# Layer 2's opening makes the keys and values of batches 1 to 3 beside batch 0's gathers; two more gather turns in the expert stage

## The chip, the cores and the metric

One core of a Trainium2 chip runs the whole program. The metric is the device time of one execution in microseconds. Engines: TensorE (PE) multiplies and transposes, VectorE (DVE) and ScalarE (ACT) do elementwise work and reductions, GpSimd (POOL) issues the indexed DMAs and small arithmetic, SyncE (SP) issues plain DMAs. Each engine works through its own queue in program order and waits on semaphores.

## The reference, cut to what matters

Two layers over x of shape (8, 256, 512), with a context of the same shape:

```python
x = x + tanh(g_xattn[0]) * causal_attention(layernorm(x), ctx, ctx)
x = x + tanh(g_ffn[0])   * mixture_of_32_experts_top8(layernorm(x))
# layer 2
q = rms_norm(layernorm(x) @ w_q.T + b_q, g_q)       # needs layer 1's x
k = rms_norm(ctx @ w_k_img.T + b_k_img, g_k_img)    # needs only ctx
v = ctx @ w_v_img.T + b_v_img                       # needs only ctx
x = x + tanh(g_xattn[1]) * (softmax(q k / sqrt(32)) v @ w_o.T + b_o)
x = x + tanh(g_ffn[1])   * (layernorm(x) @ ternary(w).T + bias)
```

In layer 2 only the 257 image tokens of the context count, so all 256 are keys and the text branch has none. There are 16 heads of 32. The point that matters here: keys and values of layer 2 depend on the context alone, queries depend on the rows that the experts produce.

## The kernel before, in words

The program has three stages, each a block; all engines meet at the end of a block (L1114, the exit of the expert stage's block).

1. Layer 1's attention and gating, batch by batch, up to about 341 us.
2. The expert stage (`experts`), up to 962.3 us: 160 tiles of 128 rows, each loaded from `x_slots`, multiplied by its expert's weights and stored to `y_tiles` in DRAM. At its end POOL starts to collect batch 0's expert rows (`add_first`): for each of a token's 8 experts one indexed DMA per 128 tokens (t = 0, 1), which adds the rows to `xs` (even turns) or to a second buffer `odd` (odd turns). A turn waits for the tile stores that it may read. Turns 0 to 3 are in the expert stage's block, turns 4 to 7 (`LAST_ADDS = 4`) open layer 2's block.
3. Layer 2 (`layer1` in the code), batch by batch, with attention written as 16 steps (two heads of one query tile in each). Work of other batches is hung beside the steps by tables that name, for each engine, which piece comes after which step: `PREP1` for the preparation of the next batch, `POST1` for the end of the batch before. Batch 0's own preparation has no attention to hide beside; its order on each engine is `BEGIN1`. I call the time from the block's start to the first attention step the opening, and the 16 steps of batch n body n.

The pieces of a preparation: `sc` splits the context into two fp16 halves, `T0 T1` transpose them on PE (16 fp16 transposes for two, L1548), `P...` are products of 12 matmuls of 128x512 (L1542) into one bank, read by DVE (L1659): keys, values, queries, for two row tiles each. `xc` is the mean and variance of the batch's rows on DVE (L1636 to L1642) and the inverse root on POOL (L1615); `xn` normalises on DVE (L1646); `sx T2 T3` split and transpose the result. `P` on ACT squares keys or queries for their RMS norm and on POOL makes the factor (L1622 to L1626), `r` scales queries (L1666), `k0..k3` split into head parts, `S0..S7` transpose them to the attention's layout (L372, copied L379). `v` is a wait only.

POOL's queue in layer 2 is in program order too: `BEGIN1["pool"]` with some of batch 1's gathers between, then in body n one gather of batch n+2 after each step (`add_rows`), and the small pieces at their steps. A gather of one t waits for the landing of the gather before it of the same t, since both add to the same rows; each t has eight in a batch. `xc` of batch n+1 stands at step 4 of body n on DVE and 5 on POOL, and waits for all gathers of batch n+1.

```python
            before = {"P1": 4, "xc": 0, "P3": 4}
            for piece in BEGIN1["pool"]:
                add_next(before[piece])
                pool_prep(pool, b0, piece)
            add_next(2 * ROWS - added[0])
```

## Time and profile before

| | |
|---|---|
| device time, median of 3 runs | 1558.1 us (1552.81 to 1558.12) |
| span of the profiled execution | 1525.3 us; its own device time is not in the records, the median lies 32.8 us above the span |
| PE, DVE, ACT, POOL busy | 86%, 64%, 60%, 34% of the span |
| mean granted TensorE clock | 0.939 |
| expert stage ends | 962.3 us |
| opening of layer 2 | 962.4 to 1022.0 us |
| body 0, 1, 2, 3 | 57.5, 62.3, 62.6, 62.4 us |

A share of busy time is a mean over stages with different limits; the opening and the bodies have to be read by themselves. The granted clock says at which of its two levels TensorE ran (1.00 is 2.4 GHz, 0.50 is 1.2 GHz).

### The profile page before, as it was taken

To read this page: it belongs to the slowest core of one execution; us is meant where nothing else is said; L and a number is where in the kernel's file an instruction comes from. 1 tells how busy PE (TensorE), PEld (TensorE's weight loads), DVE (VectorE), ACT (ScalarE), POOL (GpSimd) and SP (SyncE) were. 2 spreads that over 40 slices of the span, in tenths; PEclk is the share of its full clock that TensorE was granted. 3 is DMA by queue.
4 is the path that set the end of the run, shared out by engine and by line. 5 is a ranking of instruction groups with operands and counts; after the bars stand their busy time and mean duration, and the time that the engine had idled before them with its cause. 6 is when DMAs were issued, how large, how long until landed. Compare 5 with 4: busy or idle time off the path is not lost.

```text
span 1525.3 us, 37150 instructions
## 1 busy us (share of the span) xinstructions
PE 1309.4 (86%) x10733; PEld 834.6 (55%) x10734; DVE 972.8 (64%) x2387; ACT 920.1 (60%) x2261; POOL 520.1 (34%) x531
## 2 busy tenths in 40 slices
PE   5888888837999999999999999477989889898984
PEld 3656655524556666665666666144556555555552
DVE  5888888755456665655655633255787777776853
ACT  4777777724556666666666666244766667667661
POOL 1044444455333433332000001665554444541000
PEclk9988888968999999999999999688999999999997
DMA  2044344458888767767676545775654555642000
GB/s 72 29 173 180 146 146 151 156 213 304 269 285 282 256 219 261 238 217 244 218 242 222 181 149 154 126 111 83 98 99 65 104 82 84 100 65 52 15 1 28
DMA packets 96131, 233.39 MB, mean 153 GB/s; under 512 B 11808, under 2 KB 11808, under 8 KB 91424
## 3 DMA queue, kind: packets, MB, share of 16 engines
q0 software_dynamic: 33712, 113.79, 29.8%
q1 hardware_dynamic: 62320, 118.34, 23.3%
q8 instruction: 55, 0.90, 0.3%
q14 instruction: 44, 0.36, 0.1%
HBM read 140.84 MB, written 91.24 MB: 152 GB/s over the span
## 4 chain that ended last, share of the span: by engine, by line
PE 45%; DMA 9%; DVE 9%; issue 8%; ACT 3%; POOL 3%; SPq 1%; DVEq 0%; ACTq 0%; POOLq 0%
PE bank L1305 18%; PE bank L1329 10%; PE bank L1542 6%; DMA xs<-y_tiles,slot_ix 5%; PE bank L1293 4%; PE bank L258 2%; PE bank L1316 1%; PE bank L278 1%; DMA xg<-x_slots 1%; DVE l_nmax L325 1%; PE bank L1548 1%; POOL xs L430 1%; DMA x_slots<-blank 1%; DVE l_stack L379 1%; PE bank L240 1%
## 5 line engine op out<-in xcount | busy, mean ns | idle before, releaser
L1305 PE MATMUL bank<-wh,xT 128*128 x1280 | 343.3, 330 | 4.7 <-DVE hp L1420 4.4
L430 POOL DMA_INDIRECT xs<-y_tiles,slot_ix x120 | 194.6, 1622 | 234.2 <-DMA y_tiles<-ysb 99.1
L293 ACT ACTIVATE l_probs<-bank,l_bias 128x256 f32<-128x256 f32 (+1 forms) x512 | 224.4, 449 | 64.4 <-DVE l_bias L327 64.0
L1305 PE MATMUL bank<-wl,xT 128*128 x640 | 211.4, 330 | 0.0
L325 DVE TENSOR_REDUCE l_nmax<-bank 128x2 f32<-128x512 f32 (+1 forms) x256 | 158.1, 617 | 70.8 <-PE bank L240 41.3
L1410 DVE SCALAR_TENSOR_TENSOR hv<-bank,sg 128x192 f32<-128x192 f32 x160 | 56.9, 356 | 227.5 <-ACT sg L1364 203.5
L1379 ACT ACTIVATE ysb<-bank,xg 128x512 f32<-128x512 f32 x160 | 109.9, 687 | 119.1 <-PE bank L1329 119.1
L305 ACT ACTIVATE l_probsT<-bank 128x512 f32<-128x512 f32 (+1 forms) x256 | 140.0, 547 | 65.6 <-PE bank L278 65.2
L1358 ACT ACTIVATE xT<-bank 128x1024 f16<-128x1024 f16 x160 | 162.5, 1016 | 15.0 <-PE bank L1293 14.8
L1305 PEld LDWEIGHTS bank<-wh,xT 128*128 128x128 f16 x1280 | 126.5, 99 | 81.3 <-issue 11.1
L1329 PE MATMUL bank<-wh,hT 128*128 x480 | 156.1, 380 | 0.9 <-issue 0.9
L240 PE MATMUL bank<-l_stack 128*128 128x256 f16 (+1 forms) x512 | 105.7, 275 | 59.1 <-ACT l_probs L293 49.3
L278 PE MATMUL bank<-id,l_probs 128*128 128x128 f32 x896 | 149.7, 286 | 2.1 <-ACT l_probsT L305 0.5
L699 POOL DMA_INDIRECT x_slots<-room,slot_ix x112 | 113.4, 1013 | 108.3 <-issue 47.0
L1542 PE MATMUL bank<-w_hi,halfT 128*128 128x512 f16 x384 | 125.9, 390 | 18.9 <-DVE accb L1659 17.1
L1200 POOL DMA_DIRECT2D raw<-in_experts_dram x30 | 16.8, 560 | 334.1 <-DVE wl L1436 333.8
L1364 ACT ACTIVATE sg<-bank 128x192 f32<-128x192 f32 x160 | 52.8, 330 | 113.8 <-PE bank L1305 113.8
L1329 PE MATMUL bank<-wl,hT 128*128 x320 | 121.4, 379 | 0.0
L1293 PEld LDWEIGHTS bank<-id,xg 128*128 128x128 f16 x1280 | 84.9, 99 | 58.7 <-DMA xg<-x_slots 22.6
L1293 PE MATMUL bank<-id,xg 128*128 128x128 f16 x1280 | 98.9, 221 | 19.1 <-DMA xg<-x_slots 18.9
L278 PEld LDWEIGHTS bank<-id,l_probs 128*128 128x128 f32 x896 | 102.6, 147 | 11.7 <-ACT l_probsT L305 7.4
L1436 DVE SCALAR_TENSOR_TENSOR wl<-raw,wh x64 | 95.4, 1491 | 20.0 <-issue 15.9
(246 smaller groups left out, 2538.1 us busy)
## 6 DMA issues: line engine op xcount, KB each, us to landing
xg<-x_slots SPq DMA_DIRECT2D x160, 272.0 KB, 2.8
y_tiles<-ysb SPq DMA_DIRECT2D x160, 256.0 KB, 2.5
raw<-in_experts_dram POOLq DMA_DIRECT2D x30, 1280.0 KB, 7.1
x_slots<-blank SPq DMA_DIRECT2D x33, 272.0 KB, 3.6
xs<-in_x_dram SPq DMA_DIRECT2D x8, 512.0 KB, 4.4
cbuf<-in_ctx_dram SPq DMA_DIRECT2D x8, 512.0 KB, 5.8
stage<-in_mats_dram POOLq DMA_DIRECT2D x4, 1024.0 KB, 7.8
room<-in_ctx_dram SPq DMA_DIRECT2D x8, 512.0 KB, 4.6
```

Of the source, the lines that this page charges most:

```text
L240: last = self.nc.tensor.matmul(o, self.stack[:, b.par, 0, h, qt * P : (qt + 1) * P], self.stack[:, b.par, 1, h, 0:nk], start=True, stop=no ...
L278: last = self.nc.tensor.transpose(self.pT[s % len(self.pT)][:, (2 * kt + u) * P : (2 * kt + u + 1) * P], self.probs[:, s % 2, u, kt * P : ...
L293: last = self.nc.scalar.activation(self.probs[:, s % 2, u, 0:nk], self.pS[s % 2][:, u * S : u * S + nk], ACT.Exp, bias=self.bias[:, s % 4, ...
L305: self.nc.scalar.activation(self.probsT[:, s % 2, 0:w], self.pT[s % len(self.pT)][:, 0:w], ACT.Copy).then_inc(self.probsT_made, 1)
L325: self.nc.vector.tensor_reduce(self.nmax[:, s % 4, :], v, AX, ALU.max).then_inc(self.max_made, 1)
L430: return nc.gpsimd.indirect_dma_start(to, None, self.y_tiles[0 : (MT + 1 - k) * P, :], ix, compute_op=ALU.add)
L699: nc.gpsimd.indirect_dma_start(shared.x_slots, bass.IndirectOffsetOnAxis(ap=slot_ix[:, QT * b.n + t, k % TOPK : k % TOPK + 1], axis=0), xe ...
L1293: last = nc.tensor.transpose(o[:, c * P : (c + 1) * P], rows[:, c * P : (c + 1) * P], id16[:])
L1305: last = nc.tensor.matmul(bGU[t.place % 2][:, 0:GU], xT[:, t.place % 2, xo + c * P : xo + (c + 1) * P], wp[:, bass.ds(w, 1), c * GU : (c + ...
L1329: last = nc.tensor.matmul(bY[t.place % 2][:, :], h, wp[:, bass.ds(w, 1), at : at + H].rearrange("p a w -> p (a w)"), start=k == 0, stop=k ...
L1358: nc.scalar.activation(xT[:, t.place % 2, :], bX[t.place % 2][:, :].bitcast(F16), ACT.Copy).then_inc(x_ready, 1)
L1542: last = nc.tensor.matmul(o, xT[:, xo + c * P : xo + (c + 1) * P], w[:, c * H : (c + 1) * H], start=n == 0, stop=n == len(todo) - 1)
```

## The change

Layer 2's opening gets six row tiles of batches 1 to 3 (`EARLY = 3`): SP loads their context, ACT and DVE split it (`c0..c5`), PE transposes it (`t0..t5`) and makes the key product (`x0..x5`) and the value product (`v0..v5`) of each in banks of their own, DVE adds the bias, SP stores both to a DRAM tensor `kv`. In the preparation of batches 1 to 3 (`PREP1_EARLY`) the pieces `sc T0 T1` and four of six products go; SP loads the raw keys into `cbuf` and the values into `vbuf`, ACT squares the keys from there (`s0 s1`). Batch 0's order (`BEGIN1`) is rewritten, `xc` moves on DVE behind `v2`, and on POOL behind `P1`. `LAST_ADDS` goes from 4 to 2: turns 4 and 5 of batch 0's gathers stand in the expert stage's block. Three reads of table values in the expert stage get bounds.

```diff
-LAST_ADDS = 4
+LAST_ADDS = 2
+EARLY = 3
 BEGIN1 = dict(
-    pe=["T0", "T1", "P0", "P1", "T2", "T3", "P2", "P3", "S0", "S1", "S2", "S3", "S4", "S5", "P4", "S6", "S7", "P5", "v"],
-    act=["sc", "T0", "T1", "sx", "P0", "P1", "T2", "T3", "k0", "k1", "P2", "P3", "k2", "k3"],
-    pool=["xc", "P1", "P3"],
-    dve=["sc", "xc", "xn", "P0", "sx", "P1", "P2", "k0", "k1", "P3", "S0", "S1", "S2", "S3", "r", "k2", "k3", "S4", "S5", "P4", "S6", "S7", "P5"])
+    pe=["T0", "T1", "P0", "P1", "t0", "P2", "P3", "t1", "x0", "v0", "t2", "S0", "S1", "S2", "S3", "x1", "v1", "t3", "x2", "v2",
+        "T2", "T3", "x3", "P4", "P5", "v3", "t4", "x4", "v4", "t5", "S4", "S5", "x5", "S6", "S7", "v5", "v"],
+    act=["sc", "T0", "T1", "c0", "c1", "P0", "P1", "t0", "t1", "c2", "k0", "k1", "t2", "c3", "t3", "sx", "T2", "T3", "c4", "c5",
+         "P4", "P5", "t4", "k2", "k3", "t5"],
+    pool=["P1", "xc", "P5"],
+    dve=["sc", "c0", "c1", "P0", "P1", "P2", "P3", "k0", "k1", "c2", "x0", "v0", "S0", "S1", "S2", "S3", "x1", "c3", "v1", "x2", "v2",
+         "xc", "xn", "sx", "x3", "c4", "P4", "P5", "v3", "c5", "r", "k2", "k3", "x4", "v4", "S4", "S5", "x5", "S6", "S7", "v5"])
+PREP1_EARLY = dict(
+    pe={6: ["T2"], 7: ["T3", "P0"], 8: ["<S0", "<S1"], 9: ["<P1", "<S2"], 10: ["S3"], 12: ["S4", "S5"], 13: ["S6", "S7"], 15: ["v"]},
+    act={1: ["s0"], 2: ["s1"], 4: ["sx"], 6: ["T2"], 7: ["k0", "T3"], 8: ["k1", "P0"], 9: ["P1"], 10: ["k2"], 11: ["k3"]},
+    pool={5: ["xc"], 6: ["s1"], 11: ["P1"]},
+    dve={4: ["xc", "xn"], 6: ["sx"], 7: ["k0", "P0"], 8: ["k1", "S0", "S1"], 9: ["P1", "S2"], 10: ["S3", "r", "k2"],
+         12: ["k3", "S4", "S5"], 13: ["S6", "S7"]})
...
-                code = pe.value_load(t_pe[0:1, t.column()])
+                code = pe.value_load(t_pe[0:1, t.column()], min_val=0, max_val=E * E)
...
+            if piece[0] == "t":
+                pe.wait_ge(early_half, u + 1)
+                if u > 0:
+                    pe.wait_ge(early_copied, u)
+                turn16(bEarlyT, early16[:, u % 2, :, :]).then_inc(early_ps, 1)
+            else:
+                m = "xv".index(piece[0])
+                pe.wait_ge(early_copied, u + 1)
+                if u > 0:
+                    pe.wait_ge(kv_made, 2 * u + m - 1)
+                products(bEarly[m][:, :], earlyT[:, u % 2, :], 2 * m).then_inc(kv_ps, 1)
...
+            if piece[0] == "c":
+                dve.wait_ge(early_hi, u + 1)
+                v.scalar_tensor_tensor(early16[:, u % 2, 1, :], early_x[:, u % QT, :], SC_C, early16[:, u % 2, 0, :],
+                                       ALU.mult, ALU.subtract).then_inc(early_half, 1)
+            else:
+                m = "xv".index(piece[0])
+                dve.wait_ge(kv_ps, 2 * u + m + 1)
+                if u > 0:
+                    dve.wait_ge(kv_out[m], 16 * u)
+                v.scalar_tensor_tensor(early_out[:, m, :], bEarly[m][:, :], 1.0 / (SC_C * SC_W), vec[:, 2 * m, :],
+                                       ALU.mult, ALU.add).then_inc(kv_made, 1)
...
+            def load(n):
+                sp.wait_ge(at.parts_ready, 4 * n)
+                if early(n):
+                    for m in range(2):
+                        sp.wait_ge(kv_out[m], 16 * QT * n)
+                    sp.dma_start(cbuf[:, :, :], kv[n - 1, 0]).then_inc(ctx_in, 16)
+                    if n >= 2:
+                        sp.wait_ge(at.out_made, 2 * (n - 1))
+                    sp.dma_start(vbuf[:, n % 2, :, :], kv[n - 1, 1]).then_inc(v_in, 16)
+                else:
+                    sp.dma_start(cbuf[:, :, :], cv[n]).then_inc(ctx_in, 16)
...
-            before = {"P1": 4, "xc": 0, "P3": 4}
+            before = {"P1": 0, "xc": 0, "P5": 4}
...
+            pe.wait_ge(early_copied, EARLY_TILES)
+            pe.wait_ge(kv_made, 2 * EARLY_TILES)
```

The last two waits stand between the opening and the first attention step. SP issues all twelve stores and waits for them before its loads of the bodies.

## Rows read from the trace of the kernel before

**Rows 1.** The page: span and busy time of PE.
```profile
span 1525.3 us, 37150 instructions
PE 1309.4 (86%) x10733; PEld 834.6 (55%) x10734; DVE 972.8 (64%) x2387; ACT 920.1 (60%) x2261; POOL 520.1 (34%) x531
```
**Rows 2.** Windows: stretch, length, busy PE PEld DVE ACT POOL, clock, DMA share, GB/s.
```profile
962.36:1022.20 59.84, 30.23 (x175) 15.72 (x176) 23.86 (x42) 14.65 (x29) 37.01 (x30) 0.71 0.70 112
1022.20:1079.70 57.50, 47.14 (x405) 30.05 (x404) 34.96 (x72) 35.14 (x103) 33.31 (x26) 0.91 0.63 96
1079.70:1142.00 62.30, 55.99 (x478) 34.52 (x476) 46.51 (x92) 41.16 (x111) 33.78 (x27) 1.00 0.56 87
1142.00:1204.60 62.60, 56.36 (x472) 35.10 (x473) 46.25 (x93) 40.81 (x111) 29.27 (x25) 0.97 0.53 85
```
**Rows 3.** POOL's gathers in time order: start, length, [idle before <- releaser].
```profile
959.80 1.53 POOL L430 DMA_INDIRECT room<-y_tiles,slot_ix  x1 [0.30 <-issue]
976.50 1.53 POOL L430 DMA_INDIRECT room<-y_tiles,slot_ix  x1 [0.30 <-issue]
986.62 1.58 POOL L430 DMA_INDIRECT xs<-y_tiles,slot_ix  x1 [0.18 <-issue]
1024.66 2.03 POOL L430 DMA_INDIRECT xs<-y_tiles,slot_ix  x1 [0.52 <-DMA xs<-y_tiles,slot_ix]
1030.82 1.55 POOL L430 DMA_INDIRECT xs<-y_tiles,slot_ix  x1 [1.78 <-ACT l_probs L293]
1042.22 1.55 POOL L430 DMA_INDIRECT xs<-y_tiles,slot_ix  x1 [1.74 <-DMA xs<-y_tiles,slot_ix]
1081.17 1.85 POOL L430 DMA_INDIRECT xs<-y_tiles,slot_ix  x1 [1.11 <-ACT l_probs L293]
```
**Rows 4.** The exit of the expert stage's block: instructions, first and last start.
```profile
L1114 PEldq EVENT_SEMAPHORE  x2: 51/51/51, 960.4 to 962.3; - x2
L1114 POOLq EVENT_SEMAPHORE  x2: 17/17/17, 962.2 to 962.2; - x2
```
**Rows 5.** PE in time order, opening and body 0.
```profile
965.06 1.89 PE L1548 MATMUL bank<-id,l_parts 128*128 128x128 f16 x16 [4.82 <-DVE l_parts L1653]
992.68 1.06 PE L1548 MATMUL bank<-id,l_parts 128*128 128x128 f16 x16
995.29 0.39 PE L1542 MATMUL bank<-w_hi,halfT 128*128 128x512 f16 x1 [1.55 <-ACT halfT L1593]
997.68 0.38 PE L1542 MATMUL bank<-w_hi,halfT 128*128 128x512 f16 x1
998.93 0.38 PE L1542 MATMUL bank<-w_hi,halfT 128*128 128x512 f16 x1 [0.87 <-DVE accb L1659]
1047.76 0.60 PE L240 MATMUL bank<-l_stack 128*128 128x256 f16 x2 [8.31 <-ACT l_probs L293]
```
**Rows 6.** DVE in time order: normalisation, first reciprocal of a body's end.
```profile
982.29 0.69 DVE L1862 TENSOR_TENSOR xs<-xs,room 128x512 f32<-128x512 f32 x1 [1.28 <-DMA room<-y_tiles,slot_ix]
986.48 1.06 DVE L1646 TENSOR_SCALAR accb<-xs,mv,rstd 128x512 f32<-128x512 f32 x2 [0.85 <-POOL rstd L1615]
1044.57 1.05 DVE L1646 TENSOR_SCALAR accb<-xs,mv,rstd 128x512 f32<-128x512 f32 x2 [8.31 <-POOL rstd L1615]
1094.95 1.00 DVE L1646 TENSOR_SCALAR accb<-xs,mv,rstd 128x512 f32<-128x512 f32 x2 [1.87 <-POOL rstd L1615]
1155.32 1.06 DVE L1646 TENSOR_SCALAR accb<-xs,mv,rstd 128x512 f32<-128x512 f32 x2
```
**Rows 7.** DMA issues from 940 us on: KB each, median us to landing.
```profile
out_dram<-outb SPq DMA_DIRECT2D x8, 512.0 KB, 2.8
room<-in_ctx_dram SPq DMA_DIRECT2D x7, 512.0 KB, 4.3
```
**Rows 8.** The bounded read of a table value on SP; PE's tile products.
```profile
L1157 SPq FUSED_REGOPS  x280: 46/152/162, 342.1 to 939.2; - x140
...
L1305 PE MATMUL bank<-wh,xT 128*128 x1280 | 343.3, 330 | 4.7 <-DVE hp L1420 4.4
```

More of the change, by code:

```diff
@@ L1633, in dve_prep_ @@
             if piece == "xc":
+                if early(b.n):
+                    chain.batch(b.n)
                 for t in range(QT):
@@ L1774, in load_next @@
-            def load_next(b):
-                sp.wait_ge(at.parts_ready, 4 * b.n + 4)
-                load(b.next())
-            sp.sem_inc(out_free, 1)
-            load_next(Batch(0, 0, 0))
-            load_next(Batch(1, 1, 0))
-            with sp.Fori(0, (B - 3) // 2) as i:
-                for k in range(2):
-                    load_next(Batch(2 * i + 2 + k, k, i + 1))
-                    store(Batch(2 * i + k, k, i))
-            for n in range((B - 3) // 2 * 2, B):
+            kv = shared.kv.rearrange("e m (t p) h -> e m p t h", p=P)
@@ new lines, in load_early, with store_early, store @@
+            def load_early(i):
+                if i > 0:
+                    sp.wait_ge(early_half, QT * i)
+                sp.dma_start(early_x[:, :, :], cv[i + 1]).then_inc(early_in, 16)
+            def store_early(u):
+                for m in range(2):
+                    sp.wait_ge(kv_made, 2 * u + m + 1)
+                    sp.dma_start(kv[u // QT, m][:, u % QT, :], early_out[:, m, :]).then_inc(kv_out[m], 16)
+            def store(n):
+                sp.wait_ge(out_ready, 2 * n + 2)
+                sp.dma_start(ov[n], outb[:, :, :]).then_inc(out_stored, 16)
+                sp.wait_ge(out_stored, 16 * n + 16)
+                sp.sem_inc(out_free, 2)
@@ L1788, in _ @@
+            load_early(0)
+            for i in range(EARLY):
+                if i + 1 < EARLY:
+                    load_early(i + 1)
+                for u in range(QT * i, QT * i + QT):
+                    store_early(u)
+            for m in range(2):
+                sp.wait_ge(kv_out[m], 16 * EARLY_TILES)
+            sp.sem_inc(out_free, 1)
+            load(1)
+            load(2)
+            for n in range(B):
                 if n + 3 < B:
-                    load_next(Batch(n + 2, n % 2, n // 2 + 1))
@@ L1790, in _ @@
-                store(Batch(n, n % 2, n // 2))
+                    load(n + 3)
+                store(n)
         @block.gpsimd
@@ L1817, in body @@
                         pool_post(pool, b.prev(), piece)
-                    for piece in pieces(PREP["pool"], s) if prep else []:
+                    for piece in pieces(prep_of(b.next())["pool"], s) if prep else []:
                         pool_prep(pool, b.next(), piece)
@@ L1840, in body @@
                         act_post(act, b.prev(), piece)
-                    for piece in pieces(PREP["act"], s) if prep else []:
+                    for piece in pieces(prep_of(b.next())["act"], s) if prep else []:
                         act_prep(act, b.next(), piece)
@@ L1878, in body @@
                         dve_post_(dve, b.prev(), piece, post)
-                    for piece in pieces(PREP["dve"], s) if do_prep else []:
+                    for piece in pieces(prep_of(b.next())["dve"], s) if do_prep else []:
                         dve_prep_(dve, b.next(), piece, prep)
```

162 lines of the change are left out of this document (106 added, 56 removed).

## The prediction

> **What bounds the kernel now.** I read the page, then windows of the third stage, then POOL, PE and DVE there in order of time. Over the span PE is busy 86% [rows 1], but not evenly. In bodies 1 and 2 it is busy 56 of 62.5 us at full clock [rows 2]: they are bound by PE's work. In the opening it is busy 30.2 of 59.8 us, part of that at the lower clock [rows 2], and body 0 has a hole: PE waits 8.3 us until 1047.8 [rows 5]. The hole comes from POOL. DVE has waited 8.3 us for `rstd` when it normalises batch 1 at 1044.57 [rows 6], and POOL stood in its queue behind gathers. So there are two resources: PE's work, and POOL's chain of gathers. That chain has its own pace. Batch 1's first gather goes at 986.62, the first of its last pair at 1024.66, seven pairs later [rows 3]: 5.43 us a pair, whatever PE does, since a gather waits for the landing of the one before it on the same rows.
>
> The change takes work from the first resource where it binds. I ask what it does to the second.
>
> **Unit prices.** A warm product of 12 matmuls runs from 995.29 to 997.68 for 11 starts, so 2.4 + 0.2 = 2.6 us; the next starts at 998.93, 0.9 us after the bank is read by DVE [rows 5]. Two turns take 1.06 us warm and 1.89 us at the lower clock [rows 5]; I take 0.53 each. Early work per batch: 2 turns and 4 products, 1.1 + 10.4 = 11.5 us; for three batches 34.4 us. It is taken from bodies 0, 1, 2 and put into the opening.
>
> **Start of the block.** Turns 4 and 5 are four more gathers on POOL at 1.53 + 0.30 us [rows 3]; they follow the one that ends at 961.3, so POOL is through at 968.7. Now all engines meet at the block's exit: PE comes at 960.4 and leaves at 962.3 with POOL [rows 4]. After the change they all wait for POOL. Its sequencer may reach the exit before its last gather is through, so the price lies between 0 and 7; I take 6: the block starts at 968.4. Batch 0's rows are not sooner complete for it, as POOL issues the same eight gathers back to back until 978.0 either way [rows 3].
>
> **To the normalisation of batch 0.** PE began 2.7 us after the block's start (965.06 [rows 5]), so 971.1. DVE's order puts `xc` behind `v2`, and PE must first do 6 turns (3.2), 10 products (26.0) and S0 to S3 (2.1): 31.3 us. To it come the lower clock after the pause (the pair of turns at 965.06 cost 1.89 for 1.06 and the first product went at that clock too: 3 us) and 3 us of gaps at single banks, three of the 0.9 kind. `v2` ends at 1008.4. DVE reads it (0.7) and needs 0.7 + 4.2 us for `xc` (982.29 to 986.48 [rows 6], and the first of the two additions): `xn` begins at 1014.1 instead of 986.5. Batch 1's first gather stands behind that on POOL: +27.7 us.
>
> **To the first attention step.** T2 can begin 2.4 us after `xn`, at 1016.5. PE has idled 8 us, so I charge 2.5 us of lower clock again. Then 4 turns (2.1), 8 products x3, P4, P5, v3, x4, v4, x5, v5 (20.8), S4 to S7 (2.1), the first scores (0.9), and gaps 3.0: 31.4 us. Attention starts at 1047.9 for 1022.0: +26. So 34.4 us of work went into an opening with some 30 us of idle PE, and most of it shows, because the order has new waits and the block starts later.
>
> **Batch 1's gathers and body 0.** On POOL four gathers follow `xc`, then comes `P5`, which waits for the squares of batch 0's queries. Those need T2, T3, x3, P4, P5 on PE, from 1016.5 about 12.3 us, and 1.5 us on DVE and ACT: POOL is past it at 1031.7, and the gather chain has stood still some 5 us. Twelve gathers remain, six pairs: the last pair begins at 1031.7 + 5 x 5.43 = 1058.9. Before, the first gather of body 0 came 6.2 us after the last pair's first (1024.66, 1030.82), step 4's at 1042.22, 11.4 us later, and `xn` 2.35 us after that [rows 3, 6]. The same steps now give 1065.1, 1076.5 and 1078.8. `xn` of batch 1 is 34.3 us later. After it the body took 1079.7 - 1044.6 = 35.1 us, and of its work only one product goes (the others stood before the hole): end at 1111.3, **+31.6 us**. The late start of the bodies costs nothing more, this wait is longer.
>
> **Bodies 1 and 2.** Eleven us each go from PE. But POOL is level with PE at the start of body 1 (1081.17 against 1079.7), and `xn` came at +15.25 in that body, pinned by the gathers (DVE waited for `rstd` [rows 3, 6]). Five gathers and `rstd` need the same 15 us again, a little later for the shorter body 0 (+0.7). Only work behind `xn` gives time back: two products and small things, 5.7 us. Body 1: -4.9. In body 2 POOL had got ahead; `xn` came at +13.3 [rows 6]. It gets less ahead when body 1 is shorter; I take +11.2, so 2.1 before and 5.7 behind `xn`: -7.8. Body 3 onward is as before.
>
> **The rest.** SP's 12 stores: a store lands in 2.8 us [rows 7], and the two products of a tile lie 5.2 us apart, so the next write of the buffer doesn't wait. The last store and the load of batch 1's keys (2.8 + 4.3 us [rows 7]) end about 6 us after attention starts; ACT, whose `s0` stands at step 1, waits for them with its exponentials queued behind. This hides under the wait for `xn`; without that cover it would cost 5 us. Later loads are issued half a body ahead. The final store of batch 0 waits behind a load that waits for body 1's end: 3 us late, with most of a body until its buffer is wanted. Bounds on the table reads: on SP such a read has a register operation of 152 ns [rows 8]; PE waited only 4.7 us before 1280 tile products, so its sequencer runs ahead. I take 0; the bound is 160 x 0.15 = 24 us, and below zero nothing is removed.
>
> **Sum.** 31.6 - 4.9 - 7.8 = +18.9 us. On the span 1525.3 that is 1544.2; what lies around the span (32.8 us against the median) stays, so **1577 us** against a median of 1558.1. Own range: the block's start -6 to +1, the clock and gaps of the opening -4 to +4, the pairs' pace 5.0 to 5.9 us over six pairs -3 to +3, what bodies 1 and 2 give -8 to +5: about 1563 to 1589.
>
> **Rivals.**
> Gathers keep up, PE binds alone (faster). If POOL's chain has reserve, body 0's hole closes (8.3 us) and all 34.4 us leave the bodies, while the opening, PE-bound from 965 with 22 + 34.4 us of work and 9 us of clock and gaps, ends at 1030.5, +8.5. That is -34, 1524 us. It decides at `xn` of batch 1: it must come within 10 us of the first attention step. For it: PE idles half of the opening. Against it: the pair's pace and the waits for `rstd` [rows 3, 6]. The Trainium skill's Perfetto Trace Analysis (Identifying Performance Opportunities, Optimization Strategy) says that where the most contended engine changes over time, interleaving those regimes may help; this change does just that, and by that rule this rival is the one to bet on. The trace agrees that there are two regimes, but shows the gathers still running under the bodies. Chance 0.07.
>
> Late start, all given back (no change). The opening goes as I say, pairs run at 5.0 us (-5), and bodies 1 and 2 give the full 11.4 us each: 31.6 - 5 - 22.8 = +4, 1562 us. For it: POOL was ahead of PE by body 2. Against: body 1 began level. Chance 0.10.
>
> The sequencers are late in the expert stage. If half of the 24 us for bounds shows in the 160 tiles, 1589 us; all of it 1601. For it: PE and DVE read a value in every tile. Against: no PE gaps there [rows 8]. Chance 0.08.
>
> The forecast keeps 0.75. A measurement of this kernel tells about 0.5% (8 us) from no change. Faster is the first rival, 0.07; within 0.5% the second, 0.10; slower 0.83. For 8 in 10 the range starts at the second rival, 1562, and ends a little past the third's half price, 1590.
>
> **What would show it.** The trace after should have: PE, ACT and DVE leaving the block's exit near 968 with POOL; `xn` of batch 0 near 1014; the first attention step near 1048; a PE hole of some 20 us in body 0 ended by `rstd`, with `xn` of batch 1 near 1079; body 0 ending near 1111; bodies 1 and 2 of 57 and 55 us; bodies from 3 on at 62 us; an expert stage of unchanged pace. If `xc` of batch 0 is ready well before 1008, or body 0 has no hole, or bodies 1 and 2 fall to 51 us, the forecast is wrong in that step. If the exit waits for nothing on POOL, everything is about 6 us earlier.

## The result: 44 us slower, 2.8%

| | before | after |
|---|---|---|
| median of the runs | 1558.0 us (1552.8 to 1558.1, 4 runs) | 1602.2 us (1592.8 to 1608.1, 4 runs) |
| ratio after to before | | 1.0285, 95% interval 1.0252 to 1.0317 |
| profiled execution: span | 1525.3 us | 1601.3 us (its own time 1603.1) |

The direction was forecast, the size was not: 1577 us, with a range up to 1590. To read the spans: layer 1's stage took 341 us in the profiled execution of before and 374 us in that of after, with the same code. Of the kernels below, the four of group 2, all on one chip, show about 340 us and all others 370 to 377. In after the device time lies 1.8 us above its span, so before's span of 1525.3 belongs to a time near 1527, and not, as the prediction took it, to 1558 with 32.8 us around it. The slip cancels, since the forecast is a difference. By stages, each from its own trace (a body ends at DVE's reciprocal):

| stage, us | before | after | difference | forecast |
|---|---|---|---|---|
| layer 1 (same code) | 341.3 | 374.4 | +33.1 | 0 |
| expert stage with its exit | 621.1 | 631.0 | +9.9 | +6.0 |
| layer 2's start to the end of body 0 | 117.3 | 146.4 | +29.1 | +25.6 |
| body 1 | 62.3 | 63.4 | +1.1 | -4.9 |
| body 2 | 62.3 | 58.1 | -4.2 | -7.8 |
| bodies 3 to 6 | 242.7 | 249.4 | +6.7 | 0 |
| body 7 and tail | 78.2 | 78.5 | +0.3 | 0 |

Without layer 1 the differences make +42.9 us; the medians differ by 44.2.

The page of after, to be held against [rows 1]:

```profile
span 1601.3 us, 37800 instructions
...
PE 1329.1 (83%) x10733; PEld 844.4 (53%) x10734; DVE 975.4 (61%) x2387; ACT 924.0 (58%) x2261; POOL 518.0 (32%) x531
```

Windows of after (columns as in [rows 2]): the opening up to batch 0's normalisation and from there to the first attention step, body 0, body 1 in three parts (up to its normalisation, the 15 us behind it, the rest), body 2, body 3.

```profile
1005.40:1050.80 45.40, 34.24 (x200) 17.14 (x200) 18.99 (x33) 13.21 (x19) 9.79 (x11) 0.88 0.43 109
1050.80:1085.00 34.20, 27.96 (x166) 14.58 (x167) 16.54 (x28) 10.82 (x22) 17.53 (x14) 0.89 0.60 110
1085.00:1151.80 66.80, 39.31 (x341) 26.34 (x340) 31.07 (x66) 32.45 (x100) 36.71 (x29) 0.77 0.68 113
1151.80:1168.10 16.30, 8.08 (x82) 5.33 (x80) 7.28 (x19) 8.51 (x25) 9.12 (x7) 0.88 0.64 115
1168.10:1183.00 14.90, 12.34 (x95) 8.05 (x96) 9.45 (x19) 10.63 (x27) 8.97 (x8) 0.79 0.64 89
1183.00:1215.20 32.20, 27.72 (x241) 17.74 (x238) 25.97 (x50) 18.42 (x53) 13.92 (x13) 0.95 0.53 84
1215.20:1273.30 58.10, 47.46 (x408) 30.86 (x408) 42.63 (x86) 38.66 (x108) 30.14 (x25) 0.94 0.60 102
1273.30:1334.20 60.90, 54.90 (x472) 34.33 (x472) 46.02 (x92) 40.70 (x110) 29.28 (x25) 1.00 0.53 87
```

And two windows of before, body 1 ahead of its normalisation and behind it:

```profile
1079.70:1095.00 15.30, 14.47 (x127) 9.19 (x126) 9.70 (x23) 10.29 (x26) 9.17 (x7) 1.00 0.61 89
1095.00:1142.00 47.00, 41.51 (x352) 25.34 (x350) 36.80 (x70) 30.87 (x85) 24.61 (x20) 1.00 0.54 86
```

Body 0 behind the normalisation of batch 1, before and then after, and body 1 of after behind its normalisation in one piece:

```profile
1044.57:1079.70 35.13, 30.55 (x277) 20.67 (x278) 26.28 (x53) 25.87 (x78) 19.66 (x17) 0.87 0.62 98
...
1117.00:1151.80 34.80, 28.81 (x265) 19.68 (x266) 25.06 (x51) 24.81 (x75) 19.38 (x17) 0.86 0.63 99
1168.10:1215.20 47.10, 40.06 (x332) 25.79 (x332) 35.41 (x68) 29.05 (x79) 22.89 (x20) 0.90 0.56 85
```

Three things are to be seen. PE's busy time in the opening rose from 30.2 [rows 2] to 34.2 + 28.0 = 62.2 us, +32.0, as meant. In bodies 0, 1 and 2 it fell by 7.8, 7.9 and 8.9 us, 24.6 in all and not 34.4, because the same work takes longer at a lower granted clock: 0.77, 0.79 to 0.95 and 0.94 in these bodies, for 0.91, 1.00 and 0.97 before [rows 2]. (Busy time times clock, an estimate, falls by some 35 us.) And in body 1 most of the work taken away stood *ahead* of the normalisation: PE is busy 8.1 of 16.3 us there for 14.5 of 15.3, while the part behind it takes 14.9 + 32.2 = 47.1 us for 47.0.

The exit of the expert stage's block in after, which answers to [rows 4]:

```profile
L1126 PEldq EVENT_SEMAPHORE  x2: 51/51/51, 998.1 to 1005.4; - x2
L1126 ACTq EVENT_SEMAPHORE  x2: 17/17/17, 999.0 to 1005.3; - x2
L1126 POOLq EVENT_SEMAPHORE  x2: 17/17/17, 1005.2 to 1005.3; - x2
```

PE arrives at 998.1 and leaves with POOL 7.3 us later; before it waited 1.9 us.

POOL's queue in after [rows 3]: batch 0's inverse root, the gathers round P5, the root of batch 1. In brackets the idle time before, and its releaser.

```profile
1050.06 0.70 POOL L1705 TENSOR_TENSOR rstd<-mv,neghalf 128x2 f32<-128x2 f32 x1 [28.57 <-DVE mv L1734]
...
1059.56 1.56 POOL L442 DMA_INDIRECT xs<-y_tiles,slot_ix  x1 [1.86 <-DMA xs<-y_tiles,slot_ix]
1067.25 0.19 POOL L1712 TENSOR_SCALAR ss<-ss 128x2 f32<-128x2 f32 x1 [6.13 <-ACT junk L1690]
...
1114.65 1.54 POOL L442 DMA_INDIRECT xs<-y_tiles,slot_ix  x1 [1.53 <-DMA xs<-y_tiles,slot_ix]
1115.64 1.32 POOL L1705 TENSOR_TENSOR rstd<-mv,neghalf 128x2 f32<-128x2 f32 x1
```

DVE's normalisations of batches 0 to 3 in after [rows 6]:

```profile
1050.80 1.04 DVE L1738 TENSOR_SCALAR accb<-xs,mv,rstd 128x512 f32<-128x512 f32 x2 [0.81 <-POOL rstd L1705]
1117.00 1.00 DVE L1738 TENSOR_SCALAR accb<-xs,mv,rstd 128x512 f32<-128x512 f32 x2 [10.75 <-POOL rstd L1705]
1168.09 1.00 DVE L1738 TENSOR_SCALAR accb<-xs,mv,rstd 128x512 f32<-128x512 f32 x2 [7.80 <-POOL rstd L1705]
1226.35 1.00 DVE L1738 TENSOR_SCALAR accb<-xs,mv,rstd 128x512 f32<-128x512 f32 x2 [2.65 <-POOL rstd L1705]
```

The end of batch 0, worked off in body 1, has pieces of its own (`POST1`): b0 b1 split the attention output of the two row tiles on DVE, c0 c1 transpose it on PE, d0 d1 are its products. PE in after [rows 5]: behind batch 0's normalisation, the first attention step, and in body 1 the post piece c1:

```profile
1053.28 1.89 PE L1578 MATMUL bank<-id,l_parts 128*128 128x128 f16 x16 [7.88 <-DVE l_parts L1745]
...
1084.86 0.38 PE L250 MATMUL bank<-l_stack 128*128 128x256 f16 x2 [0.98 <-DVE outb L1621]
...
1170.63 1.01 PE L1578 MATMUL bank<-id,a 128*128 128x128 f16 x8 [9.90 <-DVE a L1823]
```

The same place in before: the last matmul of product P2 of the preparation, then c1. DVE's normalisation there starts at 1094.95 [rows 6].

```profile
1096.34 0.38 PE L1542 MATMUL bank<-w_hi,halfT 128*128 128x512 f16 x1
1097.50 0.61 PE L1548 MATMUL bank<-id,a 128*128 128x128 f16 x8 [0.78 <-DVE a L1731]
```

ScalarE in body 0 of after, squaring the keys that came back from DRAM (loaded at 1087.77, landed 6.9 us later):

```profile
1094.67 0.63 ACT L1690 ACTIVATE junk<-room 128x512 f32<-128x512 f32 x1 [6.96 <-DMA room<-kv]
```

### The profile page after: what moved, and what is told of

Same layout as the page of the kernel before. It is cut to its first block and busy times, and to the rows that moved or that the text cites. A ratio compares the mean times of both kernels' runs of the same rounds, so it can differ in the third digit from the quotient of the medians.

```text
span 1601.3 us, 37800 instructions
## 1 busy us (share of the span) xinstructions
PE 1329.1 (83%) x10733; PEld 844.4 (53%) x10734; DVE 975.4 (61%) x2387; ACT 924.0 (58%) x2261; POOL 518.0 (32%) x531
## 5 line engine op out<-in xcount | busy, mean ns | idle before, releaser
L442 POOL DMA_INDIRECT xs<-y_tiles,slot_ix x120 | 190.7, 1589 | 243.2 <-DMA y_tiles<-ysb 99.1
L1317 PEld LDWEIGHTS bank<-wh,xT 128*128 128x128 f16 x1280 | 126.2, 99 | 82.9 <-issue 13.9
L288 PE MATMUL bank<-id,l_probs 128*128 128x128 f32 x896 | 155.0, 293 | 2.7 <-ACT l_probsT L315 0.5
L250 PEld LDWEIGHTS bank<-l_stack 128*128 128x128 f16 x512 | 45.7, 102 | 143.6 <-ACT l_probs L303 100.8
L288 PEld LDWEIGHTS bank<-id,l_probs 128*128 128x128 f32 x896 | 106.4, 151 | 15.1 <-ACT l_probsT L315 10.3
```

Source lines behind the costliest of these rows:

```text
L250: last = self.nc.tensor.matmul(o, self.stack[:, b.par, 0, h, qt * P : (qt + 1) * P], self.stack[:, b.par, 1, h, 0:nk], start=True, stop=no ...
L288: last = self.nc.tensor.transpose(self.pT[s % len(self.pT)][:, (2 * kt + u) * P : (2 * kt + u + 1) * P], self.probs[:, s % 2, u, kt * P : ...
L442: return nc.gpsimd.indirect_dma_start(to, None, self.y_tiles[0 : (MT + 1 - k) * P, :], ix, compute_op=ALU.add)
L1317: last = nc.tensor.matmul(bGU[t.place % 2][:, 0:GU], xT[:, t.place % 2, xo + c * P : xo + (c + 1) * P], wp[:, bass.ds(w, 1), c * GU : (c + ...
```

## The experiments

Eighteen kernels ran, in five groups; a group shares its chip and its runs of before. "Over before" is the difference of the medians of one group, since the time of before was 1522.5 us on the chip of the second group and 1553 to 1559 on the others. The stages are from each kernel's trace, one execution each. Every kernel that starts from before has the bounded reads too.

| kernel | over before, us | ratio and interval | expert stage | start to end of body 0 | body 1 | body 2 | bodies 3 to 6 |
|---|---|---|---|---|---|---|---|
| bounds_only | +2.9 | 1.0018 (0.9996 to 1.0039) | 619.7 | 118.6 | 61.9 | 62.4 | 243.3 |
| after_again | +38.7 | one run | 630.5 | 145.2 | 64.4 | 58.7 | 246.4 |
| turns_late | +32.1 | 1.0201 (1.0163 to 1.0240) | 624.7 | 144.5 | 62.6 | 58.0 | 246.2 |
| norm_early | +19.9 | 1.0134 (1.0087 to 1.0180) | 624.9 | 127.2 | 64.2 | 58.9 | 244.3 |
| before_rstd | +25.1 | 1.0145 (1.0120 to 1.0170) | 627.5 | 115.0 | 65.2 | 65.0 | 256.5 |
| after_rstd | +35.1 | 1.0227 (1.0211 to 1.0243) | 628.6 | 143.4 | 56.5 | 57.3 | 256.7 |
| first_rstd | +33.0 | 1.0204 (1.0176 to 1.0233) | 636.1 | 135.0 | 57.7 | 57.0 | 253.6 |
| first_rstd_keys | +26.1 | 1.0152 (1.0125 to 1.0179) | 634.5 | 132.9 | 57.0 | 57.9 | 256.6 |
| before_first_body | +6.3 | 1.0033 (1.0016 to 1.0049) | 627.5 | 115.8 | 61.2 | 60.9 | 246.1 |
| early_tuned | +19.1 | 1.0123 (1.0101 to 1.0144) | 626.5 | 125.3 | 61.0 | 57.1 | 245.8 |
| early_tuned_late | +15.2 | 1.0092 (1.0072 to 1.0112) | 623.3 | 124.7 | 61.3 | 57.2 | 248.2 |
| early_one | +15.4 | 1.0100 (1.0076 to 1.0124) | 624.0 | 116.9 | 69.8 | 62.4 | 243.0 |
| chain_before | +1.4 | 1.0003 (0.9987 to 1.0019) | 626.5 | 110.6 | 62.2 | 60.9 | 244.5 |
| chain_after | +25.6 | 1.0167 (1.0151 to 1.0182) | 628.9 | 132.5 | 63.1 | 57.8 | 246.3 |
| chain_early | +6.1 | 1.0038 (1.0022 to 1.0054) | 624.1 | 120.2 | 61.6 | 57.2 | 245.9 |
| chain_one | +13.4 | 1.0090 (1.0071 to 1.0110) | 623.8 | 121.1 | 69.0 | 62.4 | 245.7 |
| ahead_after | +31.0 | 1.0191 (1.0156 to 1.0227) | 626.6 | 137.5 | 63.4 | 58.3 | 243.2 |
| ahead_early | +21.1 | 1.0136 (1.0098 to 1.0173) | 628.2 | 132.7 | 62.1 | 57.3 | 242.4 |

### Group 1: the bounds, the turns, the place of batch 0's normalisation

bounds_only is before with the three bounded reads and nothing else; after_again is after once more.

```diff
-                code = pe.value_load(t_pe[0:1, t.column()])
+                code = pe.value_load(t_pe[0:1, t.column()], min_val=0, max_val=E * E)
```

> The kernel before, with only the three bounded table reads of the change. Theory (gather chain and opening): layer 1's attention stage and the expert stage are not what the change slows by its design; the trace of after has its expert stage 4.6 us longer and layer 1's stage 33.1 us longer than the profiled execution of before, but that execution (span 1525.3) is shorter than the timed runs of before suggest. So this kernel runs at 1558 to 1563 us, 0 to 5 us for the bounds, and its trace, near 1556 to 1561 us, shows layer 1's stage ending near 374 us as in after, not at 341. Rival (the bounds or the changed instruction stream cost the time): 1590 us or more, with layer 1's stage at 374 us and the expert stage 5 us longer. If the trace ends layer 1 at 341 us and the time is 1558, the 33 us belong to something else in the change.

> The kernel after, unchanged, for a second trace. Theory: opening and body 0 to 2 repeat within 1 us (block exit 5.4 us after the last expert rows' turn begins as in the first trace, xn of batch 1 near 135 us after batch 0's first gather), while the 7 us that bodies 4 to 6 had more than before (clock 0.95 to 0.97 in them) vary from execution to execution. Rival: they repeat, and are a cost of the change.

The bounds cost nothing that can be told (1.0018, at most 6 us by the interval), and the rival of late sequencers, which needed 31 us or more, is out. bounds_only also serves as before with layer 1 at 373 us. after_again repeats bodies 0 to 2 to about 1 us; of the +6.7 us of bodies 3 to 6 it shows 3.7.

turns_late undoes the two turns (`LAST_ADDS = 4` in after):

> After with turns 4 and 5 of batch 0's gathers back in layer 2's block (LAST_ADDS = 4). Theory: the block starts 5 to 6 us earlier, and since batch 0's normalisation stands behind v2 on DVE and not behind the rows, all that follows is 5 to 6 us earlier: 1596 to 1597 us. Rival (the rows of batch 0 set the normalisation, so their turns pay): the same time as after or slower, 1602 us or more.

```profile
L1126 PEldq EVENT_SEMAPHORE  x2: 51/51/51, 999.5 to 1001.1; - x2
...
L1126 POOLq EVENT_SEMAPHORE  x2: 17/17/17, 1000.9 to 1001.0; - x2
```

PE now waits 1.6 us at the exit for 7.3. Expected were 5 to 6 us less; measured are 11 between the medians, which come from different chips, and 6.6 against after_again's single run on the same chip. Over all traces the expert stage takes 624.6 us on average with four turns outside (11 traces) and 629.7 with two (9): 5.1 us.

norm_early moves `xc`, `xn` on DVE from behind v2 to behind P3, and puts 14 gathers ahead of P5 on POOL:

```diff
-    dve=["sc", "c0", "c1", "P0", "P1", "P2", "P3", "k0", "k1", "c2", "x0", ..., "v2", "xc", "xn", "sx", ...
+    dve=["sc", "c0", "c1", "P0", "P1", "P2", "P3", "xc", "xn", "k0", "k1", "c2", "x0", ..., "v2", "sx", ...
-            before = {"P1": 0, "xc": 0, "P5": 4}
+            before = {"P1": 0, "xc": 0, "P5": 14}
```

> After with xc and xn of batch 0 on DVE behind P3 instead of behind v2, and 14 of batch 1's 16 gathers ahead of POOL's P5 instead of 4. No work is added or removed. Theory (batch 1's gathers are started too late, then the bodies wait for them): batch 1's first gather goes some 25 us earlier, the hole in body 0 (DVE waits 10.8 us for rstd) and PE's 7.9 us before T2 go, attention starts about 9 us earlier, and bodies 1 and 2 fall to 52 to 55 us: 1602 - 9 - 28 - 12 = about 1553 us (1540 to 1565). Rival (PE's added work in the opening is the cost, 34 us for which the bodies give nothing back because ACT and DVE are the next bound): 1590 us or more, with bodies 1 and 2 still near 60 us.

```profile
1026.93 1.04 DVE L1738 TENSOR_SCALAR accb<-xs,mv,rstd 128x512 f32<-128x512 f32 x2 [0.81 <-POOL rstd L1705]
1094.92 1.06 DVE L1738 TENSOR_SCALAR accb<-xs,mv,rstd 128x512 f32<-128x512 f32 x2 [0.84 <-POOL rstd L1705]
1144.82 1.00 DVE L1738 TENSOR_SCALAR accb<-xs,mv,rstd 128x512 f32<-128x512 f32 x2 [7.80 <-POOL rstd L1705]
```

Batch 0's normalisation comes 20 us sooner (+25.6 from the block's start for +45.4), the hole of body 0 is gone (0.84 us), and body 0 ends 19 us sooner. These are two edits at once; chain_after below takes the gathers alone. But the expected 1553 us was missed by 26, and the rival's 1590 by 11. Attention starts at +79, as in after: behind batch 0's normalisation PE is busy 43.6 of 53.4 us at a clock of 0.90, so its own work now fills most of the opening. Body 1, expected at 52 to 55 us, still waits 7.8 us for the root and still takes 64 us.

### Group 2: the place of the root on POOL

In before the variance of batch 1 is there at 1034.6 and the root only at 1044.5, behind gathers that it does not need. The same edit in three kernels, `xc` on POOL from step 5 to step 2; first_rstd is norm_early with it, and first_rstd_keys also loads batch 1's keys sooner on SP.

```diff
-    pool={5: ["xc"], 7: ["P1"], 11: ["P4"]},
+    pool={2: ["xc"], 7: ["P1"], 11: ["P4"]},
```

> The kernel before (with bounded table reads, which cost nothing measurable: 1562 against 1559) with one position changed: POOL makes batch n+1's inverse root (xc) ahead of the gather of step 2 of a body and no longer behind those of steps 2 to 4. In the trace of before, the variance is there at 1034.6 and the root is made at 1043.8, ten us later, behind gathers that it does not need. Theory A (the wait for rstd is a place in POOL's queue, not the landing of gathers): body 0's hole of 8 to 9 us closes, xn of batch 1 comes some 2 us after the variance, body 0 falls from 61.9 to about 53, and bodies 1 on stay at 61 to 62: 1551 us, ratio 0.995. Rival B (the chain of gathers is the bound, as the prediction had it): the gathers of batch 2 start later for standing behind the root, body 1's xn comes as many us later in its body, and the time stays within 2 us of 1560.

> The kernel after with the same one move, in both tables (xc on POOL at step 2). Theory A: body 0 gives back about 8 us and body 1, whose xn waited 7.8 us for the root, about 6, body 2 about 2: 1602 - 16 = 1586 us. Rival B (gathers' pace pins the normalisation, so the saved PE work of bodies 1 and 2 cannot show): unchanged, 1598 to 1602. Rival C (body 0's hole is the wait of ScalarE for the keys' round trip through DRAM): body 0 unchanged, body 1 shorter by 6: 1594.

> The version of norm_early (batch 0's xc and xn ahead of the early tiles, 14 gathers ahead of P5) with xc on POOL at step 2. There body 0 had no wait for the root any more (0.8 us), body 1 had 7.8 us. Theory A: body 0 unchanged at 48, body 1 from 64.2 to about 57, body 2 from 58.9 to about 56: 1579 - 9 = 1570. Rival B: body 1 and 2 unchanged, 1579.

> first_rstd, and the load of batch 1's keys is issued after the stores of its own tiles and the two of batch 2 (SP's queue), no longer behind the last store of all twelve. In the trace of norm_early ScalarE waits for that load until 1086.5 in step 1 of body 0, DVE 4.3 us and PE 3.5 and 4.3 us behind it. Theory C (that wait is on the path once the gathers are not): another 6 to 7 us from body 0, 1564. Rival D (body 0 is then held by something else, the landing of batch 1's gathers or the root): within 2 us of first_rstd.

before_rstd was expected 8 us faster and came out 25 us slower. A later body of it, POOL and then ACT:

```profile
1160.65 0.71 POOL L1615 TENSOR_TENSOR rstd<-mv,neghalf 128x2 f32<-128x2 f32 x1 [12.09 <-DVE mv L1642]
```
```profile
1176.28 0.72 ACT L349 ACTIVATE l_parts<-accb,rs 128x512 f16<-128x512 f32 x1 [4.05 <-POOL rs L1626]
```

POOL reaches the root early and stands 12.1 us, since its queue is in order. The gathers that it passed are issued later and stand in front of the next piece, the keys' factor; ScalarE waits 4.1 us for that, and bodies 1 to 5 grow from 61 or 62 to 65 us. Theory A fell as a general rule. For body 1 of after it held: 63.4 became 56.5 us. The windows of after_rstd, body 1 ahead of its normalisation and behind it:

```profile
1112.90:1122.20 9.30, 8.05 (x81) 5.29 (x79) 7.25 (x19) 8.38 (x25) 3.69 (x3) 1.00 0.67 141
1122.20:1169.40 47.20, 39.71 (x332) 25.71 (x332) 35.59 (x69) 29.27 (x81) 28.74 (x23) 0.93 0.62 97
```

The 7 us are all ahead of xn, 9.3 us for 16.3: the place of the root is what kept the work removed there from showing. Behind xn the body takes 47.2 us, as in before (47.0) and after (47.1), though the wait for the root is only 0.84 us. In body 0 of after_rstd, xn of batch 1 comes 9.5 us sooner (+56.7 behind that of batch 0 for +66.2) and the rest takes 41.4 us for 34.8: the hole moved to other pieces (ScalarE waits 3.0 and 5.4 us for them).

In time, after_rstd is +35.1 over before for +44.2, 9 us and not the 16 expected: bodies 3 to 6, which have the same move, took 7 back. first_rstd has bodies 1 and 2 at 57.7 and 57.0 as expected, yet is +33.0 over before, where norm_early was +19.9: the same move cost it 8 us up to the end of body 0 and 9 us in bodies 3 to 6, and its expert stage is 11 us longer, without a cause that I can show. The sooner load of the keys brought 2 us up to the end of body 0 in the trace. The medians differ by 6.9 us, near the 6 to 7 expected, but the intervals of the two ratios overlap, so its worth stays open.

### Group 3: pieces moved only where they are late, and EARLY = 1

```diff
+PREP1_FIRST = dict(PREP1, pool={2: ["xc"], 5: ["P1"], 11: ["P4"]})    # before_first_body, body 0 alone
-    pool={2: ["xc"], 6: ["s1"], 11: ["P1"]},
+    pool={2: ["s1", "xc"], 9: ["P1"]},                                # early_tuned, early batches
```

early_tuned is first_rstd_keys with the old order given back to the later bodies and, for the early batches, the keys' factor (`s1`) set ahead of the root; early_tuned_late has `LAST_ADDS = 4` as well; early_one also `EARLY = 1`, with the pieces t2 to v5 gone.

> The kernel before, and only for body 0 POOL makes batch 1's inverse root ahead of the gather of step 2 and its factor for the keys (P1) ahead of the gather of step 5; all later bodies keep their order. In before_rstd the root at step 2 in every body took 8 us of hole out of body 0, but 5.5 us came back there as ScalarE's wait for that factor (5.64 us, POOL behind three gathers), and each later body grew from 61.2 to 65 us by the same wait (4.05 us), because POOL stood 12 us for a variance that is made at +12. Theory A (places in POOL's queue): body 0 at about 54, later bodies 61 to 62, 8 us less than before: ratio 0.995. Rival B (the chain of gathers binds body 0): the hole comes back at another piece and the time is within 3 us of before.

> first_rstd_keys (+26 us against before) with the order of later bodies as in before (xc on POOL at step 5 from batch 4 on) and, for the early batches, the keys' factor (s1) beside the root at step 2 and the queries' (P1) at step 9 for 11. Theory A: bodies 3 to 6 give back about 3.7 us each, 14 us, and body 0 and 1 another 5 (ScalarE's waits of 1.7 and 5.4 us for what POOL and DVE make): +7 us against before. Rival B (gathers' pace): bodies 0 to 2 unchanged at 51, 57, 58, +12. What remains in either case is the opening, some 25 us longer, and the block's exit 5 us later.

> early_tuned with LAST_ADDS = 4, so that turns 4 and 5 of batch 0's gathers stand in layer 2's block again. In the trace of after PE, ACT and SP arrive at 998 to 1000 at the block's exit and leave at 1005.3 with POOL. If that wait is on the path: 5 us less than early_tuned. If batch 0's gathers are (its rows are complete at the same time either way): no change, since the early tiles fill the time but the normalisation comes no sooner.

> The same as early_tuned_late with EARLY = 1: only batch 1's two tiles are made in the opening, batches 2 and 3 are prepared as before. 11.5 us of work go into an opening that has some 29 us of idle PE, and most of that lies ahead of batch 0's rows. Theory A (a third of the work fits in the idle time, three thirds do not): the opening grows by at most 3 us, body 0 falls by 8 us for the order on POOL and some 3 more for the work taken out: 8 us less than before, ratio 0.995. Rival B (what binds the opening is the order of its pieces, not the amount): +5 us or more, like the other early versions.

before_first_body: the root comes 10 us sooner, the keys' factor is in time, and then the queries' factor is late; the hole came back a third time, at the next small piece (ACT):

```profile
1102.23 0.63 ACT L350 ACTIVATE l_parts<-accb 128x512 f16<-128x512 f32 x1 [7.86 <-DVE accb L1667]
```

So the hole moved, as rival B said: opening and body 0 give only 2.8 us. The time, +6.3 us, is above rival B's 3 as well; layer 2 is 2 us shorter than in bounds_only's trace, and the expert stage 8 us longer. In early_tuned bodies 3 to 6 went back to 245.8 us from 256.6, as expected, but the time missed both theories (+19 for +7 or +12). Body 1 went back from 57.0 to 61.0 us, with xn at +15.2 again: DVE waits 3.1 us for the landing of batch 2's last rows, and then 3.0 us for the root, which now stands behind `s1`. The stages of its trace make some 10 us over before; the other 9 us of the medians I can't place. early_tuned_late is 3.9 us lower, near the 5 expected. early_one was expected 8 us faster and is +15. It failed in part by an error of mine: I had left P5's factor behind 14 gathers:

```profile
1059.49 1.01 PE L382 MATMUL bank<-id,l_parts 128*128 128x128 f16 x8 [17.64 <-issue]
```

ScalarE waited 14.2 us for what that factor scales, and PE 17.6.

### Group 4: the start of the chain

Here POOL issues some of batch 1's gathers before batch 0's root, while it would stand idle (28.6 us in after, 7.7 in before). Nothing else changes in chain_after, and in chain_before only the bounded reads; chain_early is early_tuned_late and chain_one is early_one with the same, the latter with four gathers ahead of P5.

```diff
-            before = {"P1": 4, "xc": 0, "P3": 4}      # chain_before
+            before = {"P1": 4, "xc": 3, "P3": 4}
-            before = {"P1": 0, "xc": 0, "P5": 4}      # chain_after
+            before = {"P1": 2, "xc": 10, "P5": 4}
```

> The kernel after with one line changed: twelve of batch 1's gathers are issued before batch 0's inverse root (2 ahead of P1, 10 ahead of xc), where POOL stood idle for 28.6 us, and only four behind it. Theory A (the start of the chain is what makes body 0's hole and pins body 1): xn of batch 0 unchanged at +45 from the block's start, xn of batch 1 follows the first attention step by 12 to 15 us in place of 32, about 17 to 20 us earlier, body 1 and 2 at 58 or less: after - 25, that is +19 us against before, ratio 1.012. Rival B (the chain is not the cause; ScalarE's wait for the keys' round trip, or PE's own work, holds body 0): at most 8 us less than after, ratio 1.023.

> The kernel before with three of batch 1's gathers issued ahead of batch 0's inverse root, in the 7.7 us that POOL stood idle. Theory A: the whole chain is 8 us earlier, so body 0's hole of 8 to 9 us goes without coming back at another piece, because the gathers around the pieces are earlier too: body 0 at 54 for 62 from its first attention step, bodies 1 on unchanged: 8 us less than before, ratio 0.995. Rival B (as in before_rstd and before_first_body, the hole moves to another piece): within 3 us of before.

> early_tuned_late (+15 us against before) with three gathers ahead of the inverse root of batch 0. Its opening is bound by PE's work, so body 0 gains nothing; the chain is 8 us ahead in bodies 1 and 2, whose xn came at +15.2 and +10.3. Theory A: body 1 from 61.3 to about 55, body 2 to 56: +8 us against before, ratio 1.005. Rival B: unchanged at +15, since PE's work and the chain are level there.

> EARLY = 1 with three gathers ahead of the inverse root and four, not fourteen, ahead of P5. In early_one P5's factor stood behind fourteen gathers, and PE waited 17.6 us for it in the opening. Theory A (room in the opening for a third of the early work): first attention step within 5 us of before's, xn of batch 1 some 5 us sooner, body 0 short; body 1 about 62: 10 us less than before, ratio 0.994. Rival B (the chain of gathers takes back what the early work gives): as chain_before or up to 3 us above it.

```profile
1054.13 1.06 DVE L1738 TENSOR_SCALAR accb<-xs,mv,rstd 128x512 f32<-128x512 f32 x2 [0.83 <-POOL rstd L1705]
1103.25 1.06 DVE L1738 TENSOR_SCALAR accb<-xs,mv,rstd 128x512 f32<-128x512 f32 x2 [0.83 <-POOL rstd L1705]
1154.21 1.00 DVE L1738 TENSOR_SCALAR accb<-xs,mv,rstd 128x512 f32<-128x512 f32 x2 [7.92 <-POOL rstd L1705]
```

In chain_after batch 1's normalisation follows that of batch 0 by 49.1 us for 66.2, its wait for the root is 0.83 us for 10.75, and body 0's end comes 13.9 us sooner; the ratio fell from 1.0285 to 1.0167. This is one line in POOL's queue, and no other edit of one kind gave as much but norm_early's (19 us), which starts the same chain sooner. So the late start of the chain behind batch 0's normalisation was the cause in body 0. Body 1 kept its 7.9 us wait and its 63 us where theory A had 58, so the whole gave 19 us and not 25.

chain_before took 8.0 us out of layer 2's opening and body 0 in its trace (110.6 for 118.6), exactly as expected, with no hole at another piece. The timed runs show no more than 1.5 us of that against bounds_only (+1.4 for +2.9), within the intervals; its profiled execution has an expert stage of 626.5 us for 619.7, with the same code. So the gain in that stage is seen, and in the time it is not. This may be more than scatter: of the eleven traces with four turns outside, the two whose layer 2 is that of before have the shortest expert stages (621.1 and 619.7), and the nine with a changed layer 2 have 623.3 to 628.2. No run tests whether it is chance. chain_early is the best of the early versions (+6.1, near theory A's +8), but by luck: bodies 1 and 2 are unchanged, and the gain (4.5 us) is in the opening and body 0, where none was expected. chain_one was expected 10 us faster and is +13.4: POOL stood 17.6 us for P5's squares with the chain behind it. In it and in early_one body 1 takes 69 to 70 us, since POOL still has seven gathers to issue in that body ahead of the root and xn comes at +20.9.

### Group 5: eight gathers ahead of the steps

```diff
-            add_next(2 * ROWS - added[0])
+            add_next(2 * ROWS + 8 - added[0])
...
-                    if b.n + 2 < B:
+                    if added[0] < B * ROWS:
```

> chain_after, and POOL issues eight of batch 2's gathers before body 0 as well, so that the chain stays eight gathers ahead of the steps in every later body. Theory A (what pins xn of batch 2 is that its sixteen gathers are tied to body 0's sixteen steps, at 2.7 us each, whatever PE has to do): xn of batch 2 comes at +9 to +11 in body 1 in place of +16.4, body 1 at 57 for 63.1, body 2 at 56 for 57.8: 8 us less than chain_after, ratio 1.011. Rival B (the pins of bodies 1 and 2 are on other engines): unchanged, 1.017.

> chain_early (ratio 1.004) with the same eight gathers ahead. Theory A: xn of batch 2 from +15.3 to +9.3 or so, bodies 1 and 2 at 56 us each for 61.6 and 57.2, body 3 back at 61: 8 us less than chain_early, ratio 0.999, level with before. Rival B: unchanged, 1.004.

Both fell: bodies 1 and 2 stay, and body 0's end is 5 and 12.5 us later. DVE in ahead_early:

```profile
1100.14 1.05 DVE L1738 TENSOR_SCALAR accb<-xs,mv,rstd 128x512 f32<-128x512 f32 x2 [11.69 <-POOL rstd L1705]
1150.99 1.04 DVE L1738 TENSOR_SCALAR accb<-xs,mv,rstd 128x512 f32<-128x512 f32 x2 [7.51 <-POOL rstd L1705]
```

The root of batch 1 stands behind eight gathers more and is waited for 11.7 us (0.8 in chain_early). And batch 2's normalisation comes at +16.4 in body 1 of ahead_after, at +16.4 in chain_after, +16.3 in norm_early, +16.3 in after and +15.3 in before: when the chain started, and how far ahead it is, makes no difference there. In all of them POOL issues the gathers of that body's first five steps ahead of the root. With two of them ahead (after_rstd, first_rstd, first_rstd_keys) it comes at +9.3; early_tuned has two ahead as well and still +15.2, for the late rows and the `s1` named above. So, apart from that, it is the place of the root within the body that counts. The number of gathers since the chain began does not: from batch 2's first gather to its normalisation it is 64.1 us in before (1030.82 [rows 3] to 1094.95 [rows 6]) and 64.8 in after (1103.26 to 1168.09), but 60.8 to 71.7 over all kernels with the same 21 gathers ahead of the root. Part of these gathers wait for attention steps and not for the landing of another (9 of 21 in before, 11 of 21 in chain_after).

## Why the prediction was right and wrong

**Block's start: right.** +6 was taken; PE waits 7.3 us at the exit for 1.9, and turns_late gives it back. The stage itself came out another 4 to 5 us longer in after's trace; other traces of the same code differ by as much.

**Opening and body 0: right to 3.5 us, up to the last term.** From the block's start: normalisation of batch 0 at 45.7 by the forecast, 45.4 measured; first attention step 79.5 and 79.5; P5's stall 5 and 6.1; normalisation of batch 1 110.4 and 111.6; end of body 0 142.9 and 146.4. The pairs of gathers behind P5 ran at 5.76 us (1068.66 to 1097.46 for five) where I had 5.43. The last term fell short: behind xn the body took 34.8 us, 0.3 less than before (35.1), where I had taken off a whole product (32.5). It is the same slip as in body 1, below. The clock does not explain it: 0.86 behind xn for 0.87 before; the low mean of body 0 (0.77) comes from the wait ahead of xn. norm_early and chain_after show the cause of the +29 itself: start the chain sooner, and 19 and 14 us of this come back.

**The keys' round trip: right that it was covered.** They landed 9.8 us after the first attention step, not 6, under the wait for `rstd`. In norm_early, where that cover was gone, ScalarE waited 3.1 us for it.

**Body 1: the step that failed.** The forecast read: "Only work behind `xn` gives time back: two products and small things, 5.7 us." The pin was right: xn came at +16.3 where I had +16. But behind it nothing was saved, 47.1 us for 47.0. Two things were wrong in that term. First its size: in before P2 was half done when xn began, so what stood behind xn was 7 of its 12 matmuls and P5, 4.1 us and not 5.7; the other 7.4 us went ahead of xn. Second, that it comes back in full. P2 had run on PE in the 2.5 us between xn and the post piece c1, which waits for DVE's xn and b1; in after PE stands idle there, and c1 follows xn by 2.5 us as before. From c1 to the end of the body it is 44.6 us for 44.5, with P5 gone but a granted clock of 0.92 for 1.00. In PE's books: busy 40.1 us for 41.5, so of the 4.1 us some 2.6 went to the lower clock and 1.5 became idle time.

Is it the wait for the root that eats the saving? Ahead of xn yes: in after_rstd, where the wait is 0.84 us, xn comes 7 us sooner and body 1 takes 56.5. Behind xn no: there it takes 47.2 us too, and in all kernels but before_rstd 45.8 to 48.9, with the early work or without. What sets those 46 to 49 us, besides the clock, no run isolates.

**Body 2: the same step.** -4.2 for -7.8. xn came at +11.1 where I had +11.2; behind it the body took 47.0 us for 49.0 before, 2.0 us saved for the 5.7 of the forecast. I also had POOL's queue wrong in one place: in body 1 POOL stands 7.5 us (5.4 before) at step 10 for the variance of the post piece d1, with the gathers of the next batch behind it. A late xn makes d1 late, and d1 the chain; no run moved it.

**Bodies 3 to 6: taken as 0, measured +6.7.** after_again and turns_late have +3.7 and +3.5, before_first_body, which has none of the early work, +3.4. About half is the spread of these bodies between executions; for the rest I have no cause.

**The sum.** Of the 25 us that the forecast lacked, 3.9 are in the expert stage, 3.5 in body 0, 6.0 in body 1, 3.6 in body 2 and 6.7 in the later bodies; the rest lies between traces and medians. The terms that I had priced from the chain of gathers held to a few per cent. Those that I had priced as work saved behind xn, 2.6 us in body 0 and 5.7 each in bodies 1 and 2, gave 0.3, 0 and 2.0.

**The rivals.** That PE binds alone and the gathers keep up did not happen: they went on under the bodies, as said. So the rule on interleaving regimes that spoke for that rival (the Trainium skill, Perfetto Trace Analysis, Optimization Strategy) does not carry this kernel: with the chain started sooner, the best early version is still 6 us above before (chain_early). That the sequencers are late is excluded by bounds_only. "All given back" needed pairs at 5.0 us and 11.4 us from each of bodies 1 and 2. The pairs took 5.76, and the bodies gave -1.1 and 4.2: what was removed ahead of xn hung on the place of the root, and what was removed behind it went to the clock and to idle time.

**A version that beats both** did not come out: chain_before is level with before (1.0003) and bounds_only within its interval; all others are slower.

## What to carry to other kernels

Before work is moved out of a stage, cut each of its bodies at the wait that ends last and count the removed work on either side. What stood ahead of the wait does not come back while the wait stays. What stood behind it comes back only if the engine had no gap there that the work had filled, and if its clock holds; here almost none of it did. In an in-order queue that also carries a paced chain of transfers, count the transfers between the stage's start and each small piece. Moving one piece forward makes the next one late, as in before_rstd and before_first_body. Starting the chain sooner, in idle time, did better where the chain had started late (chain_after, body 0). Compare stages of equal code first: here they differed by 33 us (layer 1) and 16 us (the expert stage) between chips and executions, more than most of the effects sought.

## What was not expected of the hardware

Layer 1's stage took 339.6 to 341.3 us in five profiled executions and 370.4 to 376.6 in fifteen, with one code, and before's median was 1522.5 us on the chip of the second group and 1553 to 1559 elsewhere. The expert stage took 619.7 to 636.1 us. Neither has a cause that I can show. The granted clock fell where PE had stood: 0.77 over body 0 of after, 0.79 in the 15 us behind the wait of body 1, where before had 1.00. There the long wait cost its length and some of what followed.
